# Perceiver block on one core: exponential and maximum of the cross-attention read the same score banks in turn, or two banks each at once

## What is computed

```python
k = ctx @ Wk.T + bk          # (32, 1601, 256), 16 heads of 16
v = ctx @ Wv.T + bv
q = (norm(x) @ Wq.T + bq) / 4
s = q @ k.T                  # per head: 64 queries x 1601 keys
p = exp(s - s.max(keys)); o = (p @ v) / p.sum(keys)
x = x + o @ Wo.T + bo
```

## Time and profile before

| | us |
|---|---|
| median of 3 runs (2126.26 to 2132.22) | 2128.44 |
| the profiled execution, its own time | 2133.82 |
| span of that execution | 2132.0 |
| TensorE busy | 1976.3 |
| VectorE busy | 1314.6 |
| ScalarE busy | 1049.9 |
| GpSimd busy | 614.4 |

### The profile page before, as it was taken

One profiled execution on the slowest core, in us unless ns is written; L12 is line 12 of the kernel. 1 busy time (PEld: TensorE's weight loads), 2 busy tenths in 40 slices (PEclk: granted clock), 3 DMA queues, 4 the chain that ended last, 5 costly groups with the idle time before them and its releaser, 6 DMA issues.

```text
span 2132.0 us, 72414 instructions
## 1 busy us (share of the span) xinstructions
PE 1976.3 (93%) x31796; PEld 1590.1 (75%) x31796; DVE 1314.6 (62%) x2276; ACT 1049.9 (49%) x1532; POOL 614.4 (29%) x997
## 2 busy tenths in 40 slices
PE   5798999999999999999999989999999998999987
PEld 4577777777778787787778778787787776778764
DVE  2557656856666566666666576665666666566644
ACT  3455445555455555555555544555544444444441
POOL 3322323323233232323323232332323222122201
PEclk8999999999999999999999999999999999999999
DMA  5533434243333333424333324242342321213122
GB/s 184 182 125 119 145 117 138 102 135 128 121 117 114 122 132 117 146 91 159 112 129 124 123 93 162 77 158 90 120 135 85 119 70 61 77 52 105 49 71 69
DMA packets 124469, 243.90 MB, mean 114 GB/s; under 512 B 13952, under 2 KB 44800, under 8 KB 124160
## 3 DMA queue, kind: packets, MB, share of 16 engines
q1 hardware_dynamic: 123568, 239.23, 34.0%
q10 hardware_dynamic: 592, 0.04, 0.0%
HBM read 235.94 MB, written 3.15 MB: 112 GB/s over the span
## 4 chain that ended last, share of the span: by engine, by line
PE 73%; DVE 12%; ACT 7%; issue 5%; POOL 2%; DMA 0%; SPq 0%; POOLq 0%; DVEq 0%; ACTq 0%
PE M L805 11%; PE M L812 11%; PE SC L1023 9%; PE SC L1046 8%; PE O L1067 7%; PE X L862 5%; ACT probT L1269 4%; DVE mx L1612 4%; PE SC L1039 3%; PE M L862 3%; PE X L1133 2%; PE X L1107 1%; PE M L867 1%; PE X L841 1%; PE M L906 1%
## 5 line engine op out<-in xcount | busy, mean ns | idle before, releaser
L1612 DVE TENSOR_REDUCE mx<-SC 128x4 f32<-128x1600 f32 (+1 forms) x256 | 466.8, 1823 | 145.2 <-PE SC L1023 142.1
L1269 ACT ACTIVATE probT<-SC 128x2048 f32<-128x2048 f32 (+1 forms) x256 | 398.8, 1558 | 165.4 <-PE SC L1046 164.9
L654 POOL TENSOR_TENSOR rowsT<-raw,rowsT 128x384 fp32r<-128x384 f32 (+1 forms) x256 | 279.6, 1113 | 394.4 <-ACT rowsT L1323 394.2
L812 PE MATMUL M<-wvs,rowsT 128*128 128x256 f32 x2496 | 358.6, 293 | 2.3 <-ACT kT L1208 1.4
L805 PE MATMUL M<-rowsT,wks 128*128 128x400 f32 (+1 forms) x1536 | 342.7, 364 | 11.6 <-DVE V L1414 4.8
L1208 ACT ACTIVATE kT<-M,bk 128x400 f32<-128x400 f32 (+1 forms) x256 | 151.5, 593 | 382.8 <-PE M L805 382.4
L805 PEld LDWEIGHTS M<-rowsT,wks 128*128 128x128 f32 x1536 | 271.8, 191 | 86.2 <-issue 64.4
L812 PEld LDWEIGHTS M<-wvs,rowsT 128*128 128x128 f32 x2496 | 315.1, 192 | 22.6 <-issue 2.5
L1414 DVE TENSOR_TENSOR V<-M,bv 128x512 f32<-128x512 f32 (+1 forms) x224 | 145.3, 649 | 278.0 <-PE M L812 269.8
L1023 PE MATMUL SC<-kT,bdq 32*128 32x400 f32 (+1 forms) x2048 | 244.9, 546 | 27.7 <-ACT probT L1269 23.0
L1067 PEld LDWEIGHTS O<-probT,V 128*17 128x17 f32 x13312 | 195.0, 99 | 79.7 <-issue 75.2
(11 more groups left out here) (275 smaller groups left out, 2461.3 us busy)
## 6 DMA issues: line engine op xcount, KB each, us to landing
ring<-in_ws_dram SPq DMA_DIRECT2D x428, 256.0 KB, 4.6
summed<-in_ctx_dram SPq DMA_DIRECT2D x60, 800.5 KB, 4.6
raw<-in_ctx_dram SPq DMA_DIRECT2D x64, 384.0 KB, 4.5
raw<-in_ctx_dram SPq DMA_DIRECT2D x32, 512.0 KB, 4.0
ring<-rounded_scratch SPq DMA_DIRECT2D x64, 256.0 KB, 4.0
raw<-in_ctx_dram SPq DMA_DIRECT2D x32, 321.0 KB, 4.7
out_dram<-x SPq DMA_DIRECT2D x16, 128.0 KB, 2.2
kT<-in_ctx_dram SPq DMA_DIRECT2D x2, 800.5 KB, 8.9
```

What stands on the lines that cost most here:

```text
L654: pool.tensor_tensor(rowsT[1][:, c, at], raw[:, c, at], rowsT[0][:, c, at], ALU.subtract).then_inc(low_ready, 1)
L812: mm = pe.matmul(bank[:, (t - 2 * a) * D:(t - 2 * a + 1) * D], rowsT[xp][:, cc, t * P:(t + 1) * P], wvs[wp][:, cc, :], start=(at == cc == ...
L1269: act.activation(probT[step % 3][0:w, :, 0:len(ts), :].rearrange("p j t q -> p j (t q)"), SC[0:w, :, 0:len(ts) * P], ACT.Exp)\
L1612: dve.tensor_reduce(mx[c][:, :, n], SC[:, :, 0:KCH[n][1]], AX.X, ALU.max).then_inc(max_used, 1)
```

## The change

The slot's scores are cut in two halves `h` of two key tiles (groups 3 keep one half). One block holds, in the same four banks, the scores of two tiles in columns 0 to 255 and the maxima of 256 keys in columns 256 to 511, for a block ten further on. A half `c` has 7 blocks, a batch 14. Once a block is filled (`block_filled`), ScalarE takes the exponential of banks 0 and 1 while VectorE reduces banks 2 and 3; then each waits for the other (`exp_half`, `max_half`) and they change places. The next block waits for both. The first block of a slot stands where the scores stood, the second where the maxima stood. On VectorE the reductions of the first block stand ahead of the drains of "first", and on ScalarE the second exponential stands behind the drains of `B`. The key chunks `KCH` become 512, 512, 256 and 321 columns, and the context pieces `PIECES` 4, 4, 2 and 3 tiles, with other fills to wait for. The core of the diff:

```diff
 KF = KEYS // P
 KR = KEYS - KF * P
 KP = KT * P
-NCH = (KEYS + 511) // 512
-KCH = [(KEYS * n // NCH, KEYS * (n + 1) // NCH - KEYS * n // NCH) for n in range(NCH)]
+KCH = [(lo * P, min(hi * P, KEYS) - lo * P) for lo, hi in ((0, 4), (4, 8), (8, 10), (10, KT))]
 NQ = len(KCH)
+HALF = 2 * P
+HALVES = (KEYS + HALF - 1) // HALF
 NTG = (KT + 3) // 4
 VF = (KT + 1) // 2
 STEPS = C * NQ
-LEAD = 6
+BLOCKS = C * HALVES
+LEAD = 10
 E, EH = 8, 128
...
 
 EARLY = {-17: [key(0, 0), key(0, 1)], -16: [key(1, 0), key(1, 1)], -15: [key(0, 2), key(1, 2)], -12: [value(0), value(1)], -9: [key(0, 3)], -8: [key(1, 3)], -7: [value(2)], -6: [value(3)], -5: [value(4)], -4: [value(5)], -3: [value(6)]}
 
-FIRST_WARM = (1, 2, 3, 4)
+FIRST_WARM = (2, 4, 6, 8)
 OWN = value(4), value(5), value(6)
 
...
 
 LOAD_AT = (1, 2, 3, 5)
 
-PIECES = [(0, 4, key(1, 1)), (4, 7, key(1, 2)), (7, 10, value(4)), (10, KT, value(VF - 1))]
+PIECES = [(0, 4, (key(1, 0), value(1))), (4, 8, (value(2),)), (8, 10, (value(4),)), (10, KT, (value(VF - 1),))]
 
 
...
     return step // 2 + 1
 
 
-def max_step(b, k):
-    s = STEPS * b + k + LEAD
-    return s if 0 <= s < STEPS * B else None
+def halves(k):
+
+    return 1 if k % NTG == NTG - 1 else 2
+
+
+def block_at(b, k, h):
+
+    i = BLOCKS * b + k // NTG * HALVES + 2 * (k % NTG) + h
+    return i, i + LEAD
+
+
+def half_tiles(k, h):
+
+    lo = 4 * (k % NTG) + 2 * h
+    return range(lo, min(lo + 2, KT))
+
+
+def max_chunk(j):
+
+    mb, n = divmod(j, BLOCKS)
+    c, n = divmod(n, HALVES)
+    return mb, c, n, n * HALF, min(KEYS - n * HALF, HALF)
 
 
 def full(t):
...
         bdq = [sp.sb(f"bdq{s}", [P, C, 2, S]) for s in range(2)]
         probT = [sp.sb(f"probT{n}", [P, 4, 4, 2 * S]) for n in range(3)]
         wk, wv = (probT[n].rearrange("p a b q -> p (a b q)")[:, 0:C * D].rearrange("p (c f) -> p c f", c=C) for n in range(2))
-        mx = [sp.sb(f"mx{c}", [P, 4, NQ]) for c in range(C)]
+        mx = [sp.sb(f"mx{c}", [P, 4, HALVES]) for c in range(C)]
         nmx = [sp.sb(f"nmx{c}", [P, 4]) for c in range(C)]
         mrest = sp.sb("mrest", [P, 4])
         mparts = [sp.sb(f"mparts{c}", [P, 4, 32], BF16) for c in range(C)]
...
                         pe.matmul(X.rearrange("p (a t) -> p a t", a=4), identb[:, :], identb[:, :].unsqueeze(1).to_broadcast([P, 4, P]),
                                   start=True, stop=True, skip_group_check=True)
 
-                def maxima(b, k):
-                    s = max_step(b, k)
-                    if s is None:
-                        return
-                    mb, c, n = s // STEPS, s % STEPS // NQ, s % NQ
-                    k0, kn = KCH[n]
-                    if s in FIRST_WARM:
-                        warm(2)
-                    if s % STEPS == 0:
+                def maxima(j):
+                    mb, c, n, k0, kn = max_chunk(j)
+                    if n == c == 0:
                         pe.wait_ge(bd_ready, mb + 1)
-                    wait_drained(pe, (mb, "key", n, c))
-                    if s:
-                        pe.wait_ge(max_used, s)
-                    if b >= 0:
-                        pe.wait_ge(exp_ready, STEPS * b + k + 1)
-                    for j in range(4):
-                        r = slice(32 * j, 32 * j + 32)
-                        mm = pe.matmul(SC[:, j, 0:kn], bdq[mb % 2][r, c, :, :].rearrange("p e q -> p (e q)"),
+                    for a, (lo, w) in enumerate(KCH):
+                        if lo <= k0 < lo + w:
+                            wait_drained(pe, (mb, "key", a, c))
+                    for q in range(4):
+                        r = slice(32 * q, 32 * q + 32)
+                        mm = pe.matmul(SC[:, q, HALF:HALF + kn], bdq[mb % 2][r, c, :, :].rearrange("p e q -> p (e q)"),
                                        keys(mb, c)[r, k0:k0 + kn], start=True, stop=True, skip_group_check=True)
-                    mm.then_inc(max_filled, 1)
-
-                def scores(b, k):
-                    c, g = k // NTG, k % NTG
-                    step = STEPS * b + k
-                    pe.wait_ge(max_used, min(STEPS * b + k + LEAD, STEPS * B))
-                    if step:
-                        pe.wait_ge(exp_ready, step)
-                    if g == 0:
+                    return mm
+
+                def scores(b, k, h):
+                    c = k // NTG
+                    if k % NTG == h == 0:
                         x_is_used(pe, f"max{c}", b)
-                    ts = list(tiles(g))
-                    for j in range(4):
-                        r = slice(32 * j, 32 * j + 32)
-                        w = held(ts[0])
-                        pe.matmul(SC[0:w, j, 0:len(ts) * P].rearrange("p (t q) -> p t q", q=P), sel[r, 0:w],
+                    ts = half_tiles(k, h)
+                    w = held(ts[0])
+                    for q in range(4):
+                        r = slice(32 * q, 32 * q + 32)
+                        pe.matmul(SC[0:w, q, 0:len(ts) * P].rearrange("p (t q) -> p t q", q=P), sel[r, 0:w],
                                   mT[b % 2][c][r, :].unsqueeze(1).to_broadcast([32, len(ts), P]),
                                   start=True, stop=False, skip_group_check=True)
                     for n, t in enumerate(ts):
-                        w = held(t)
-                        for j in range(4):
-                            r = slice(32 * j, 32 * j + 32)
-                            mm = pe.matmul(SC[0:w, j, n * P:(n + 1) * P], keys(b, c)[r, t * P:t * P + w],
+                        for q in range(4):
+                            r = slice(32 * q, 32 * q + 32)
+                            mm = pe.matmul(SC[0:w, q, n * P:(n + 1) * P], keys(b, c)[r, t * P:t * P + w],
                                            bdq[b % 2][r, c, :, :].rearrange("p e q -> p (e q)"),
                                            start=False, stop=True, skip_group_check=True)
-                    mm.then_inc(score_filled, 1)
+                    return mm
+
+                def scores_and_maxima(b, k, h):
+                    i, j = block_at(b, k, h)
+                    if j < 0 or i >= BLOCKS * B:
+                        return
+                    if j in FIRST_WARM:
+                        warm(2)
+                    if j:
+                        pe.wait_ge(max_used, min(j, BLOCKS * B))
+                    if i > 0:
+                        pe.wait_ge(exp_ready, i)
+                    if i >= 0:
+                        mm = scores(b, k, h)
+                    if j < BLOCKS * B:
+                        mm = maxima(j)
+                    mm.then_inc(block_filled, 1)
 
                 def weigh(b, rounds):
                     if not 0 <= b < B:
...
                             pe.wait_ge(o_used, b + 1)
                         if c == 0:
                             wait_drained(pe, (b, "value", ts[-1] // 2, 0))
-                        pe.wait_ge(exp_ready, step + 1)
+                        pe.wait_ge(exp_ready, block_at(b, k, halves(k) - 1)[0] + 1)
                         for n, t in enumerate(ts):
                             w = held(t)
                             for hh in range(8):
...
                     mm.then_inc(x_filled, 1)
 
                 for b, k in SLOTS:
-                    if 0 <= b < B:
-                        scores(b, k)
+                    scores_and_maxima(b, k, 0)
                     for what in x_fills(b, k, "A"):
                         fill_x(what, b)
                     for what in pieces(b, k, "first"):
                         fill(half_done, head=True)
                     for what in x_fills(b, k, "B"):
                         fill_x(what, b)
-                    if k in WEIGH_FIRST:
-                        weigh(*rounds_weighed(b, k))
-                    maxima(b, k)
+                    if halves(k) > 1:
+                        scores_and_maxima(b, k, 1)
                     for what in pieces(b, k, "strips"):
                         fill(what)
-                    if k not in WEIGH_FIRST:
-                        weigh(*rounds_weighed(b, k))
+                    weigh(*rounds_weighed(b, k))
                     for what in x_fills(b, k, "C"):
                         fill_x(what, b)
                     if STEPS * b + k == min(EARLY):
...
                     act.activation(th[:, h, :], halves[:, 0, :, :], ACT.Tanh, scale=0.5).then_inc(tanh_ready, 1)
                     return act.activation(v[:, h, :], halves[:, 0, :, :], ACT.Relu)
 
-                def exps(b, k):
+                def exps(b, k, h):
+                    if not 0 <= b < B:
+                        return
                     step = STEPS * b + k
-                    ts = list(tiles(k % NTG))
+                    i, j = block_at(b, k, h)
+                    ts = half_tiles(k, h)
                     w = held(ts[0])
-                    act.wait_ge(score_filled, step + 1)
-                    if step >= 3:
+                    act.wait_ge(block_filled, j + 1)
```

(37 more changed lines are left out.)

14 lines of the change are left out of this document (7 added, 7 removed).

## The result

The changed kernel takes 2242.83 us (median of 4 runs, 2234.51 to 2252.09) against 2129.59 us of the kernel before on the same chip: ratio 1.0534, 95% interval 1.0482 to 1.0585. It is slower, as forecast, but by 113 us instead of 18, and outside the range.

The account below looks back on a forecast made before the run. TensorE, busy 1976.3 of 2132.0 us, was taken as the bound. Waits gone -58, its own work -7, new stalls +81, remaining waits +2 gave +18 us: 2146 against the median 2128.4, own range 2132 to 2183, whole range 2092 to 2190.

Parts of the forecast that it names:

- Round trip: Scores block: two ScalarE and two VectorE halves free it 1.50 us after its fill, against 1.95 to 2.10 before.
- B: Rival, handovers inside each block: dear ones make the round trip 2.0 us, +105 us, 2233; chance 0.08.
- C: Rival, PSUM reads: both engines slow each other, halves take their sum of 2.55 us, +239 us, 2367; chance 0.02.
- My estimate from the Trainium skill's "Perfetto Trace Analysis": VectorE's half reduction with PSUM overhead: 0.78 us, block 1.68 us, and a sum near +44 instead of +18.
- VectorE's backlog: Work ahead of VectorE's reduction stalls TensorE after a slot's first block: 55 us in slot 1, 81 us in all.
- A: Rival, VectorE's late work: it moves earlier, stalls come to 38 us, the kernel gets faster, -33 us, 2095; chance 0.33.
- waits on `SC` of the kernel before that go: TensorE's waits for exponential and maximum before maxima and scores: nearly all cover exceeds 1.50 us, so they go, -58 us.
- waits ahead of blocks in the new kernel: TensorE standing before a slot's next block: +81 us of stalls from late VectorE, +2 us at slots with little cover.
- things that cost nothing while covered: Added VectorE and ScalarE work, later drains and context sums: hidden, except 3 us more stalls from ScalarE's later work.
- the 13 us that I had named as the limit: TensorE's busy sum: a move by more than 13 us would show the forecast wrong.
- slots 0, 4 and 5 together 11: Stalls of TensorE from VectorE's backlog in these three slots of each batch: 11 us over the run.
- The gains: TensorE: 58 us from old waits on the scores tile that go, 7 us from fewer visits to 32-row tiles.

Follow-up runs that it names:

- run 12: run 5's kernel with first blocks of slots 1 and 6 holding scores alone, and maxima-only blocks reduced in one VectorE instruction: 2125.66 us, 0.9996.
- run 2: Changed kernel with ScalarE's copy of `mT` back ahead of the first block's exponential in slots 3 and 7: 2225.48 us, 1.0445.
- Run 1: Changed kernel with VectorE's reductions of a slot's first block moved to the very start of that slot: 2199.75 us, 1.0339.
- run 5: Changed kernel with both moves, VectorE's first-block reductions at the slot's start and ScalarE's `mT` copy ahead of the first exponential: 2193.63 us, 1.0287.
- run 8: Kernel before the change, with VectorE's reduction done three times in one slot of eight (slot 5): 2263.34 us, 1.0634.
- run 9: run 5's kernel with slot 1's first block holding scores alone, drained by ScalarE alone, and an extra maxima-only block in slot 3: 2143.58 us, 1.0064.
- Run 4: Changed kernel with eight unused 512-column matmuls into `O` added before slot 1's second block: 2243.18 us, 1.0527.
- run 7: Kernel before the change, with VectorE's reduction done twice in one slot of eight (slot 5): 2178.35 us, 1.0223.
- run 11: Changed kernel with the alternation alone undone: ScalarE takes all four banks, then VectorE reduces all four: 2303.31 us, 1.0778.

## Why the prediction was wrong in size

**Right.** *Round trip*: halves of 0.60 and 0.69 us (0.585 and 0.69 predicted), starting 0.04 to 0.08 us after the fill, block free after 1.36 us in the timeline above and 1.4 to 1.5 on average where VectorE is on time (1.50 predicted). B is out by this: its time, 2233 us, lies near the result, but by another mechanism. C is out too: 599 ns beside 585 for ScalarE and 688 for VectorE while both read PSUM. The trace agrees with what the Trainium skill says in "PSUM — Partial Sum Buffer", section "Specifications (TRN2)": the two engines read PSUM in parallel at full bandwidth while they stay off each other's bank. My estimate from the Trainium skill's "Perfetto Trace Analysis", section "Optimizing Scalar/DVE Operations", 0.78 us for a half, is not borne out; 0.688 us was measured, as the rows of before had given. *VectorE's backlog* in slot 1: 55 us predicted, 55 measured. A, the soft backlog, did not happen: 28 of 32 first blocks of slot 1 stop TensorE.

The terms of the sum beside what TensorE's rows show, waits summed by what was waited for (us). The busy sum went up by 15.0; run 12, which has nearly the same blocks at the clock of the kernel before, 0.984, has 1963.6, 12.7 less than before, so 27.7 are put down to the clock. That split is an estimate:

| term | predicted | measured |
|---|---|---|
| waits on `SC` of the kernel before that go, and busy sum at the same clock | -58 - 7 | -46.6 - 12.7 |
| waits ahead of blocks in the new kernel | +81 + 2 | +101.1 |
| waits for ScalarE's late drains, `mT` and `kT` | 0 | +19.4 + 13.9 |
| all other idle time | 0 | +0.4 |
| busy sum, by the lower clock | 0 | +27.7 |
| sum | +18 | +103.2 |

**Wrong, first step: "things that cost nothing while covered", 33 us.** I moved ScalarE's drains behind the first exponential and priced them by ScalarE's own 3 us. But this exponential now contains a wait for VectorE, and the drains inherit it. For `mT` that is 19.5 us in the two rows above, and run 2 gets 17 us back. The other part is the keys' drain `kT`, ahead of a bank `M`: 9.7 us before, 23.6 after. It makes up 10.5 us of the 24.4 in slot 7 (3.3 before), which hardly changed in runs 1, 2 and 5. One such place, slot 7 of batch 5, after and then before:

```profile
480.23 0.60 PE L1034 MATMUL SC<-kT,bdq 32*128 32x256 f32 x8
...
482.27 0.38 ACT L1295 ACTIVATE probT<-SC 65x256 f32<-65x256 f32 x1 [0.99 <-DVE mx L1641]
...
488.58 0.88 ACT L1227 ACTIVATE kT<-M,bk 128x256 f32<-128x256 f32 x2
...
489.09 0.69 PE L897 MATMUL M<-ident,n 128*128 128x128 f32 x2 [3.08 <-ACT kT L1227]
```

```profile
464.23 0.44 PE L878 MATMUL M<-ident,n 128*128 128x128 f32 x2 [1.56 <-ACT kT L1208]
```

ScalarE is done with the block 1.82 us after its fill (480.83), where the exponential alone had taken until 0.95 us after the scores; and TensorE reaches the bank 0.6 us sooner, as the maxima no longer stand between its pieces. Together that is the 1.5 us by which the wait is longer. What the rest of slot 7's idle time comes from was not tested.

**Second: the clock, a term that was not in the sum, some 28 us.** A busy sum 7 us smaller was predicted and one 15.0 larger was measured, beyond the 13 us that I had named as the limit. Half of the time at the lower level gives an upper bound for the loss, (158 - 69) / 2 = 44 us, as the clock is also low where TensorE is idle. Run 8 shows the same fall of the clock, to 0.967, with 33 us more busy time, from long stops alone and with TensorE's work unchanged.

**Third: the backlog, "slots 0, 4 and 5 together 11", 18 us.** They cost 27, and all waits ahead of blocks 101 instead of 83. I took the last VectorE instruction that lay ahead of the slot's first drain at the time of the scores; where VectorE stood idle for GpSimd or TensorE in front of an instruction that comes before the reduction in its program, I saw no backlog. Before, the same wait was harmless, as the slot's first drain had time: of the 8.5 us idle in slot 4 almost nothing was for VectorE. Run 1 moves the reduction in front of those instructions and gets 43 us, clock included.

**The gains** were 6 us too high: 58 + 7 were taken, 46.6 + 12.7 measured. Whether the 12.7 us come from records that are less drawn out or from TensorE's own work was not measured apart; run 12 has as many visits as the kernel before, so fewer visits are not the reason there.

That the backlog of slot 1 stops TensorE was forecast rightly, and it is over half of the waits ahead of blocks. The three steps and the 6 us together are the 85 us between the predicted +18 and the measured +103 of the spans. Their shares can't be added up from the runs, as each stop removed also raises the clock: run 9 gets 50 us from a place with 51.7 us of idle time.

**Open.** The clock's share rests on run 12, whose blocks are not quite the same. Run 4 was not conclusive. A version in which the work of slot 0 that makes VectorE late is itself moved or shortened was not tried.

## What to carry to other kernels

When two in-order engines hand a buffer to each other inside its round trip, the later of them sets it at every use: read at each such point where the second engine stands in its program, with its idle waits on third engines, and not its busy share. Then follow what stands behind it on both engines, for it inherits the wait. Price the long stops of TensorE above their length, by a run that lengthens one. And before giving a good idea up, leave the coupling out only where the partner is late: here two blocks of fourteen held 64 us.

## What the runs showed of the hardware

Extra stops of 1.3 us a batch cost little more than their length (clock 0.984 to 0.981), those of 3.0 us a third more (0.967): after a stop of 2.22 us the same eight matmuls took 1.11 us instead of 0.60. The time at the lower level went from 69 us in the kernel before (15 stretches) to 83 us in run 7 (18) and 151 us in run 8 (36). I had costed no clock at all. And an exponential of ScalarE and a reduction of VectorE that read different banks of PSUM at once barely slowed each other: the exponential's half took 599 ns, against 585 for 512 elements in the kernel before, and 0.60 us too where VectorE was at other work (1025.89 above), and the block was free 1.36 us after its fill, where the two in turn take 1026 + 1223 ns (run 11's means).
